# A convolution and attention-like layer pair on one core: first Toeplitz reads in sequence, channel 1's x in halves, filter weights scaled ahead

## The chip, the cores and the metric

One core of a Trainium2 chip. The metric is the device time of one execution in microseconds (us); before the change it is 943.02 (median of 3, 942.68 to 943.25).

## The reference

Input x is (4 images, 64 channels, 256, 256) in f32. Per channel, two layers follow each other.

```python
# layer 0: filters from a small net, separable, applied along both axes
h = sin(freq * (z @ w1 + b1)); h = sin(freq * (h @ w2 + b2)); h = sin(freq * (h @ w3 + b3))
h = (h @ wo) * decay                      # once with the X weights, once with the Y weights
k = einsum('ijk,imk->ijmk', hx, hy)       # causal 2-d convolution of x with k, by FFT
y = conv(x, k) + x * bias
# layer 1
scores = einsum('bpsd,bptd->bpst', y, y) / 16
out = batchnorm_over(b, s, d)(y + sum(scores * weights, -1, keepdims=True)) * gamma + beta
```

The sum over t of scores times weights is computed as a product of `weights` and y, then multiplied row by row with y and summed.

## The kernel before, in words

**Filters.** Three parameter transfers (`L315`) bring z, the weights, biases, frequencies and decays. TensorE makes layer 1 in two halves of 128 positions (`L645`). In each of the three layers VectorE forms `arg` of the first half from PSUM as (x + bias) * freq / 2 pi (`L780`) and ScalarE that of the second (`L506`); VectorE subtracts the nearest whole number of turns (`L788`, `L793`), ScalarE takes the sine (`L511`), and TensorE multiplies by the next weights (`L652`). A fourth product times the decay gives `filt` (`L800`). In front of each of the later products two filler matmuls (`keep_warm`, into `ps_c`, results unused) are issued, in front of the first four, and 24 after the filters are ready. SyncE stores `filt` to `pad_dram` (`L348`), waits, and reads it back as Toeplitz matrices: row p is the filter read from position p + 1 on. Channel 0 is read in two parts: S (f = 1, `first_s_landed`) and T (f = 0, `t_landed[0]`), each 128 KB (`L341`). Every other channel is one read of 256 KB (`L336`).

**Steady work.** The 4 images of a channel are 2 pairs; 64 channels make 128 steps. Every f32 operand is split in a high part (rounded by ScalarE) and a low part (subtraction, on GpSimd, or on VectorE for u). For pair n, TensorE forms U(n) (`ps_u`, x times S), Y(n) (`ps_z`, T times u) and C(n) (`ps_c`, weights times z). In step s it issues U(s-2), Y(s-3), C(s-4); each engine runs its own in-order stage with such lags. In the steps that matter here:

- SyncE issues, before the steps, xt of channel 0, w of channel 0, xt of channel 1, and after the filter store S and T; then the steps' loads: Toeplitz 1, w(1), x(0), xt(2), x(1), Toeplitz 2, and then w(2), which waits for the low part of w(0). x(n) is the x of pair n in natural layout, w(m) the layer 1 weights of channel m.
- ScalarE: xh of pairs 0 and 1 (`L548`), high parts of S (`L535`) and T (`L539`), uh(0) (`L519`), xh of pair 2, high part of Toeplitz 1, wh(0) (`L559`), uh(1), xh of pair 3, zh(0) (`L610`).
- GpSimd: xl of pair 0 (`L461`), low part of S (`L450`), xl of pair 1, low part of T (`L442`), xl of pair 2, low part of Toeplitz 1, wl(0) (`L474`), xl of pair 3, zl(0) (`L489`).
- VectorE: ul(0) (`L890`), ul(1), then z of pair 0 (`z_sb`, `L847`), which needs Y(0) and x(0).
- TensorE: U(0) needs the high part of S and xl of pair 0, U(1) xl of pair 1, Y(0) ul(0) and the low part of T; U(2) needs ul(1), the low part of Toeplitz 1 and xl of pair 2; C(0) needs wl(0) and zl(0).

Of the kernel before, what the change touches and what calls it, by code (L numbers as in the profile page):

```python
# [24 lines left out]
COL_BIAS, COL_FREQ = COL_W1 + P, COL_W1 + P + 3  # L25
COL_W2, COL_W3, COL_WO = (COL_FREQ + 1 + i * P for i in range(3))
COL_DECAY = COL_WO + P
# [9 lines left out]

WARM_FIRST, WARM_LAYER, WARM_TOEPLITZ = 4, 2, 24

# [71 lines left out]
def build(nc, x, xt, wt, params, out):  # L111
# [45 lines left out]
    with ExitStack() as ctx:  # L157
# [6 lines left out]
        def sem(name):  # L164
            return ctx.enter_context(nc.semaphore(name))
# [49 lines left out]
        filt = early[2][:, 0:PAD]  # L215
        arg, turns, part, hid = (early[3][:, i * SIDE:(i + 1) * SIDE] for i in range(4))


# [15 lines left out]
        hid_ready = sem("hid_ready")  # L234
        filt_ready = sem("filt_ready")
        filt_stored = sem("filt_stored")
        xt_landed = [sem(f"xt_landed{i}") for i in range(XR)]
# [61 lines left out]
        def z_parts(zs):  # L299
# [3 lines left out]
            return zh[:, zs.slot(2)], zl[:, zs.slot(2)]  # L303

        def u_bank(us):

            return ps_c if second_pair(us) else ps_u
# [4 lines left out]
        def _(sp):  # L312
            for start, end, landed in ((0, COL_W2, first_landed), (COL_W2, COL_DECAY, weights_landed),
                                       (COL_DECAY, NPARAM, rest_landed)):
                sp.dma_start(par[:, start:end], params[:, start:end]).then_inc(landed, 16)  # L315
# [22 lines left out]
            def load_first_toeplitz(f, landed):  # L338

                src = bass.AP(pad_dram, f * CH * PAD + 1, [[1, P], [1, SIDE]])  # L340
                sp.dma_start(toep_whole[:, 0, f, :], src).then_inc(landed, 16)  # L341

            load_xt(0, 0)
            load_w(0, 0)
            load_xt(1, 1)

# [51 lines left out]
        def _(pool):  # L398
            nc.gpsimd.memset(filt[:, 0:P], 0.0).then_inc(const_ready, 1)
            nc.gpsimd.memset(ones[:, :].bitcast(F32), 1.0 / P).then_inc(const_ready, 1)  # L400
            nc.gpsimd.memset(minus_half[:, :], -0.5).then_inc(const_ready, 1)
            nc.gpsimd.memset(everyone[:, :, 2 * P:2 * P + 2], P * BN_EPS).then_inc(const_ready, 1)
            pool.wait_ge(const_ready, 4)

# [27 lines left out]
            def stage(st):  # L432

                ms = st.trail(LAG_MEAN)
                if starts(ms) and not ending(ms, 4):
                    shift_means(ms)

                def low_toeplitz(ts, parts):
# [18 lines left out]

                if active(st):
                    wait(pool, xh_ready, st, 1)
                    r, h = st.ring(XR), st.half()  # L460
                    nc.gpsimd.tensor_tensor(xl[:, st.slot(4)], xt_sb[:, r, PAIR * h:PAIR * (h + 1), 0],  # L461
                                            xh[:, st.slot(4)].bitcast(F32), ALU.subtract)\
                        .then_inc(xl_ready, 1)

# [33 lines left out]
        def _(act):  # L498

            act.wait_ge(const_ready, 4)  # L500
            nc.scalar.activation(sine_loaded[:, :], minus_half[:, :], ACT.Sin)
            for layer in range(3):
                act.wait_ge(layer_done, 2 * layer + 2)
                if layer == 0:
                    act.wait_ge(bias_turns_ready, 1)
                nc.scalar.activation(arg[:, HALVES[1]], ps_u[:, 1, 0, 0:P], ACT.Identity,  # L506
                                     bias=bias_turns[:, layer:layer + 1], scale=freq_turns[:, 0:1])\
                    .then_inc(second_arg, 1)
                for i, half in enumerate(HALVES):
                    act.wait_ge(reduced, 5 * layer + 4 + 2 * i)  # L510
                    nc.scalar.activation(hid[:, half], part[:, half], ACT.Sin, scale=TWO_PI_BELOW)\  # L511
                        .then_inc(hid_ready, 1)

            def round_u(us):

                if active(us):
                    wait(act, u_done, us, 1)
                    wait(act, y_done, us, -1)
                    nc.scalar.activation(uh[:, us.slot(2)], u_bank(us)[:, :, :, :], ACT.Copy)\  # L519
                        .then_inc(uh_ready, 1)  # L520

            def stage(st):
# [19 lines left out]
                ts = toeplitz_step(st)  # L542
                if active(st):
                    r, h = st.ring(XR), st.half()
                    if h == 0:
                        act.wait_ge(xt_landed[r], st.turn(XR) * 16)
                    wait(act, u_done, st, -3)
                    nc.scalar.activation(xh[:, st.slot(4)], xt_sb[:, r, PAIR * h:PAIR * (h + 1), 0],  # L548
                                         ACT.Copy).then_inc(xh_ready, 1)

# [79 lines left out]
        def _(pe):  # L630
# [9 lines left out]

            pe.wait_ge(const_ready, 4)
            keep_warm(WARM_FIRST)
            pe.wait_ge(first_landed, 16)
            for i, half in enumerate(HALVES):
                mm(ps_u[:, i, 0, 0:P], par[:, COL_W1:COL_W1 + P],  # L645
                   par[:, COL_ZT + half.start:COL_ZT + half.stop], True, True).then_inc(layer_done, 1)
# [123 lines left out]
        def _(dve):  # L770
# [4 lines left out]
            nc.vector.tensor_scalar(bias_turns[:, :], par[:, COL_BIAS:COL_BIAS + 3], freq_turns[:, 0:1],  # L775
                                    None, ALU.mult).then_inc(bias_turns_ready, 1)
            for layer in range(3):

                dve.wait_ge(layer_done, 2 * layer + 1)
                nc.vector.tensor_scalar(arg[:, HALVES[0]], ps_u[:, 0, 0, 0:P],  # L780
                                        par[:, COL_BIAS + layer:COL_BIAS + layer + 1],
                                        freq_turns[:, 0:1], ALU.add, ALU.mult).then_inc(reduced, 1)
                for i, half in enumerate(HALVES):
                    if i == 0:
                        dve.wait_ge(reduced, 5 * layer + 2)
# [4 lines left out]
                    dve.wait_ge(reduced, 5 * layer + 3 + 2 * i)  # L790
# [6 lines left out]
            dve.wait_ge(const_ready, 4)  # L797
            for i in range(2):
                dve.wait_ge(layer_done, 7 + i)
                nc.vector.tensor_tensor(filt[:, P + P * i:P + P * (i + 1)], ps_u[:, i, 0, 0:P],  # L800
                                        par[:, COL_DECAY + P * i:COL_DECAY + P * (i + 1)], ALU.mult)\
                    .then_inc(filt_ready, 1)
# [248 lines left out]
```

## Time and profile before

| | |
|---|---|
| median of the runs | 943.02 us |
| profiled execution, its own time | 943.65 us |
| its span | 941.8 us |
| busy: TensorE, VectorE, ScalarE, GpSimd | 99%, 79%, 72%, 71% |
| HBM traffic | 259 GB/s over the span |
| transfers on SyncE's queue | 85.1% of the DMA engines' span |

The span runs from the first instruction to the last. A share of busy time is a mean over the whole span; the first 30 us look different from the rest and are read by themselves below. For a transfer the profile gives the time from its issue to its landing.

### The profile page before, as it was taken

The page shows a single profiled execution, that of the slowest core. Times are in us where ns is not written, and L with a number is a line of the kernel's source. Part 1 is how long each engine was busy: PE and PEld are TensorE (multiplying, and loading weights), DVE is VectorE, ACT ScalarE, POOL GpSimd, SP SyncE. Part 2 cuts the span into 40 slices and gives each one's busy share as a digit, 9 for nine tenths or more (in the row PEclk, how much of TensorE's full clock was granted, in tenths as well). Part 3 has the DMA queues.
Part 4 walks back from the last instruction along what each step waited for, and adds up shares of the span by engine and source line. Part 5 has one row for each costly group of instructions (what it writes and reads, how often), then busy time and mean ns, then how long its engine had stood idle before and what let it go on. Part 6 is the DMA issues. An engine that isn't in the chain of part 4 may idle for free.

```text
span 941.8 us, 18640 instructions
## 1 busy us (share of the span) xinstructions
PE 928.6 (99%) x5308; PEld 812.7 (86%) x5308; DVE 740.5 (79%) x2196; ACT 680.0 (72%) x1093; POOL 672.8 (71%) x526
## 2 busy tenths in 40 slices
PE   8999999999999999999999999999999999999995
PEld 6888888888888888888888888888888888888884
DVE  2778778878878878877887887887887878888787
ACT  4447777777777777777777777777677777777777
POOL 2777777777777767777777776876777776777763
PEclk9999999999999999999999999999999999999998
DMA  7778998898999999889799999979999999988945
GB/s 231 266 223 186 289 258 271 290 238 271 258 260 285 237 284 291 292 225 288 211 289 298 209 302 291 280 236 288 215 274 311 240 269 294 262 261 293 246 152 204
DMA packets 91454, 244.15 MB, mean 259 GB/s; under 512 B 17200, under 2 KB 41904, under 8 KB 83248
## 3 DMA queue, kind: packets, MB, share of 16 engines
q1 hardware_dynamic: 73440, 235.53, 85.1%
q10 hardware_dynamic: 18000, 8.46, 3.7%
q14 instruction: 9, 0.07, 0.0%
q8 instruction: 5, 0.08, 0.0%
HBM read 176.59 MB, written 67.37 MB: 259 GB/s over the span
## 4 chain that ended last, share of the span: by engine, by line
PE 95%; DVE 2%; DMA 1%; ACT 1%; issue 1%; POOL 0%; SPq 0%; POOLq 0%; DVEq 0%
PE ps_c L632 36%; PE ps_u L632 31%; PE ps_z L632 28%; DMA toep_whole<-filters_padded 1%; DVE z_sb L847 0%; DVE products L857 0%; POOL zl L489 0%; DMA filters_padded<-z_sb 0%; DVE ul L890 0%; ACT uh L519 0%; DVE z_sb L945 0%; DVE z_sb L780 0%; DVE stat L874 0%; DVE z_sb L793 0%; ACT zh L610 0%
## 5 line engine op out<-in xcount | busy, mean ns | idle before, releaser
L489 POOL TENSOR_TENSOR zl<-z_sb,zh 128x1024 fp32r<-128x1024 f32 x127 | 304.0, 2393 | 238.5 <-ACT zh L610 238.4
L857 DVE CUSTOM_DVE_ANT_0 products<-z_sb,ps_c 128x256 bf16<-128x256 f32 x504 | 182.3, 418 | 155.1 <-PE ps_c L632 155.1
L632 PE MATMUL ps_z<-uh,toep 128*128 128x512 f32 x768 | 271.4, 408 | 0.4 <-DVE z_sb L847 0.2
L585 ACT ACTIVATE out_sb<-z_sb,shift,gain 128x256 f32<-128x256 f32 x496 | 257.2, 591 | 5.5
L519 ACT ACTIVATE uh<-ps_u 128x1024 fp32r<-128x1024 f32 x127 | 130.6, 1028 | 174.4 <-PE ps_u L632 174.4
L632 PE MATMUL ps_u<-toep,xh 128*128 128x256 f32 x1016 | 234.8, 312 | 0.8 <-DVE ul L890 0.5
L632 PE MATMUL ps_c<-zh,wh 128*128 128x512 f32 x504 | 196.2, 389 | 0.1
L632 PE MATMUL ps_c<-zl,wh 128*128 128x512 f32 x504 | 196.1, 389 | 0.0
L632 PE MATMUL ps_c<-zh,wl 128*128 128x512 f32 x504 | 196.1, 389 | 0.0
L632 PE MATMUL ps_u<-toep_whole,xt_sb 128*128 128x128 f32 x1016 | 195.1, 273 | 0.0
L610 ACT ACTIVATE zh<-z_sb 128x1024 fp32r<-128x1024 f32 x127 | 134.7, 1061 | 63.6 <-DVE z_sb L847 54.3
L461 POOL TENSOR_TENSOR xl<-xt_sb,xh 128x512 fp32r<-128x512 f32 x128 | 166.5, 1301 | 11.6 <-ACT xh L548 11.6
L632 PEld LDWEIGHTS ps_u<-toep,xh 128*128 128x128 f32 x1016 | 163.0, 191 | 11.4 <-issue 0.9
L874 DVE BATCH_NORM_STATS2 stat<-z_sb 128x6 f32<-128x512 f32 x256 | 169.6, 707 | 0.1
L632 PEld LDWEIGHTS ps_z<-uh,toep 128*128 128x128 f32 x768 | 144.4, 188 | 29.0 <-issue 0.9
L890 DVE TENSOR_TENSOR ul<-ps_u,uh 128x1024 fp32r<-128x1024 f32 x127 | 154.6, 1217 | 14.8 <-ACT uh L519 14.6
L847 DVE SCALAR_TENSOR_TENSOR z_sb<-x_sb,par,ps_z 128x1024 f32<-128x1024 f32 x128 | 163.3, 1276 | 0.0
L632 PEld LDWEIGHTS ps_u<-toep_whole,xt_sb 128*128 128x128 f32 x1016 | 157.6, 191 | 0.0
L632 PE MATMUL ps_z<-ul,toep 128*128 128x512 f32 x384 | 149.9, 390 | 0.0
L632 PE MATMUL ps_u<-toep,xl 128*128 128x256 f32 x508 | 143.8, 283 | 0.0
L632 PEld LDWEIGHTS ps_c<-zh,wh 128*128 128x128 f32 x504 | 94.6, 188 | 20.4 <-issue 0.8
L632 PEld LDWEIGHTS ps_c<-zh,wl 128*128 128x128 f32 x504 | 94.6, 188 | 19.7
(95 smaller groups left out, 907.7 us busy)
## 6 DMA issues: line engine op xcount, KB each, us to landing
xt_sb<-xt_in SPq DMA_DIRECT2D x64, 1024.0 KB, 10.8
x_sb<-x_in SPq DMA_DIRECT2D x128, 512.0 KB, 8.9
out<-out_sb SPq DMA_DIRECT2D x124, 512.0 KB, 7.3
w_sb<-wt_in SPq DMA_DIRECT2D x64, 256.0 KB, 8.0
toep_whole<-filters_padded SPq DMA_DIRECT2D x63, 256.0 KB, 8.0
everyone<-partition_moments ACTq DMA_DIRECT2D x62, 128.0 KB, 8.5
out<-z_sb SPq DMA_DIRECT2D x2, 512.0 KB, 2.6
partition_moments<-own ACTq DMA_DIRECT2D x62, 1.0 KB, 7.0
```

Of the source, the lines that this page charges most:

```text
L461: nc.gpsimd.tensor_tensor(xl[:, st.slot(4)], xt_sb[:, r, PAIR * h:PAIR * (h + 1), 0], xh[:, st.slot(4)].bitcast(F32), ALU.subtract)\
L489: nc.gpsimd.tensor_tensor(low, z_sb[:, r, h], high.bitcast(F32), ALU.subtract)\
L519: nc.scalar.activation(uh[:, us.slot(2)], u_bank(us)[:, :, :, :], ACT.Copy)\
L585: last = nc.scalar.activation(to[:, k, b], z_sb[:, r, h, k, b], ACT.Identity, bias=shift[:, r, g:g + 1], scale=gain[:, r])
L610: nc.scalar.activation(z_parts(zs)[0], z_sb[:, r, h], ACT.Copy).then_inc(zh_ready, 1)
L632: return nc.tensor.matmul(o, a, b, start=start, stop=stop)
L847: nc.vector.scalar_tensor_tensor(out=z_sb[:, r, h].rearrange("p k b w -> p (k b w)"), in0=x_sb[:, zs.slot(4)].rearrange("p k b w -> p (k b ...
L857: return nc.vector.tensor_tensor_reduce(products[:, cs.slot(2), k, b], z_sb[:, r, h, k, b], bank[:, k, b], 1.0 / math.sqrt(SIDE), 0.0, ALU ...
L874: last = nc.vector.bn_stats(stat[:, r, h * BLOCKS + k], z_sb[:, r, h, k].rearrange("p b w -> p w b"))
L890: nc.vector.tensor_tensor(ul[:, us.slot(2)], u_bank(us)[:, :, :, :], uh[:, us.slot(2)].bitcast(F32), ALU.subtract)\
```

## The change

The filters' layers 2 and 3 no longer form `arg`. GpSimd multiplies their weights by freq / 2 pi per output column (`scaled`, from a new row of frequencies in the parameters) and makes a diagonal matrix of the biases in turns (from a new identity matrix). TensorE first multiplies that diagonal with a tile of ones into the layer's PSUM bank, then adds the scaled weights' product, so PSUM holds turns, and VectorE reads it twice. The layers alternate between `ps_u` and `ps_z`. The fillers in front of layers 2 and 3 go, those in front of the output product stay, those before the Toeplitz products become 15. The second parameter transfer grows to 256 KB, the third by 64 KB.

SyncE issues half of channel 1's xt (the images of pair 2) early, and waits for S before it issues T, Toeplitz 1, the other half of xt and w(0). ScalarE and GpSimd make xh and xl of pair 2 ahead of the Toeplitz parts; GpSimd also that of pair 1.

```diff
-COL_W2, COL_W3, COL_WO = (COL_FREQ + 1 + i * P for i in range(3))
+COL_W2, COL_W3, COL_FREQ_ROW, COL_EYE, COL_WO = (COL_FREQ + 1 + i * P for i in range(5))
-WARM_FIRST, WARM_LAYER, WARM_TOEPLITZ = 4, 2, 24
+WARM_FIRST, WARM_OUT, WARM_TOEPLITZ = 4, 2, 15
...
+        row_turns, unit = (early[1][:, i * P:(i + 1) * P] for i in range(2))
+        scaled = early[1][:, 2 * P:6 * P].rearrange("p (l k n) -> p l k n", l=2, k=2)
...
+        def layer_bank(layer, i):
+            return (ps_u, ps_z)[layer % 2][:, i, 0, 0:P]
...
-            for start, end, landed in ((0, COL_W2, first_landed), (COL_W2, COL_DECAY, weights_landed),
-                                       (COL_DECAY, NPARAM, rest_landed)):
+            for start, end, landed in ((0, COL_W2, first_landed), (COL_W2, COL_WO, weights_landed),
+                                       (COL_WO, NPARAM, rest_landed)):
...
             load_xt(0, 0)
-            load_w(0, 0)
-            load_xt(1, 1)
+            load_xt_half(1, 0, early_xt_landed)
...
             load_first_toeplitz(1, first_s_landed)
+            sp.wait_ge(first_s_landed, 16)
             load_first_toeplitz(0, t_landed[0])
+            load_toeplitz(1, 1)
+            load_xt_half(1, 1, xt_landed[1])
+            load_w(0, 0)
...
-                if starts(ts) and not first_channel(ts):
+                if starts(ts) and not (ts.static() and ts.channel() < 2):
                     wait(sp, u_done, ts, -2 * XR + 2)
                     load_toeplitz(ts.channel(), ts.ring(XR))
...
+            nc.gpsimd.memset(unit, 1.0).then_inc(const_ready, 1)
...
+            pool.wait_ge(weights_landed, 16)
+            nc.gpsimd.tensor_scalar(row_turns, par[:, COL_FREQ_ROW:COL_FREQ_ROW + P], 1.0 / (2.0 * math.pi),
+                                    None, ALU.mult).then_inc(row_turns_ready, 1)
+            pool.wait_ge(row_turns_ready, 1)
+            pool.wait_ge(bias_turns_ready, 1)
+            for i, col in enumerate((COL_W2, COL_W3)):
+                nc.gpsimd.tensor_scalar(scaled[:, i, 1], par[:, COL_EYE:COL_EYE + P], bias_turns[:, i + 1:i + 2],
+                                        None, ALU.mult).then_inc(scaled_ready, 1)
+                nc.gpsimd.tensor_tensor(scaled[:, i, 0], par[:, col:col + P], row_turns, ALU.mult)\
+                    .then_inc(scaled_ready, 1)
...
+                if st.static() and st.number() == 1:
+                    low_x(st)
+                    low_x(Step(0, 2))
...
+                if st.static() and st.number() == 1:
+                    high_x(Step(0, 2))
...
-            pe.wait_ge(weights_landed, 16)
-            for layer, col in enumerate((COL_W2, COL_W3, COL_WO)):
-                keep_warm(WARM_LAYER)
+            for layer in (1, 2):
+                pe.wait_ge(scaled_ready, 2 * layer - 1)
+                for i in range(2):
+                    mm(layer_bank(layer, i), scaled[:, layer - 1, 1], unit, True, False)
+                pe.wait_ge(scaled_ready, 2 * layer)
                 for i, half in enumerate(HALVES):
-                    pe.wait_ge(hid_ready, 2 * layer + 1 + i)
-                    mm(ps_u[:, i, 0, 0:P], par[:, col:col + P], hid[:, half], True, True)\
+                    pe.wait_ge(hid_ready, 2 * layer - 1 + i)
+                    mm(layer_bank(layer, i), scaled[:, layer - 1, 0], hid[:, half], False, True)\
                         .then_inc(layer_done, 1)
+            keep_warm(WARM_OUT)
+            pe.wait_ge(rest_landed, 16)
+            for i, half in enumerate(HALVES):
+                pe.wait_ge(hid_ready, 5 + i)
+                mm(layer_bank(3, i), par[:, COL_WO:COL_WO + P], hid[:, half], True, True).then_inc(layer_done, 1)
...
             for layer in range(3):
-                dve.wait_ge(layer_done, 2 * layer + 1)
-                nc.vector.tensor_scalar(arg[:, HALVES[0]], ps_u[:, 0, 0, 0:P],
-                                        par[:, COL_BIAS + layer:COL_BIAS + layer + 1],
-                                        freq_turns[:, 0:1], ALU.add, ALU.mult).then_inc(reduced, 1)
                 for i, half in enumerate(HALVES):
+                    if layer == 0:
...
+                        whole = arg[:, half]
                     else:
-                        dve.wait_ge(second_arg, layer + 1)
-                    nc.vector.tensor_scalar(turns[:, half], arg[:, half], ROUND_MAGIC, ROUND_MAGIC,
+                        dve.wait_ge(layer_done, 2 * layer + 1 + i)
+                        whole = layer_bank(layer, i)
+                    nc.vector.tensor_scalar(turns[:, half], whole, ROUND_MAGIC, ROUND_MAGIC,
                                             ALU.add, ALU.subtract).then_inc(reduced, 1)
...
-                    nc.vector.tensor_tensor(part[:, half], arg[:, half], turns[:, half], ALU.subtract)\
+                    nc.vector.tensor_tensor(part[:, half], whole, turns[:, half], ALU.subtract)\
                         .then_inc(reduced, 1)
```

## Rows read from the trace of the kernel before

**Rows 1.** The page: TensorE's and other engines' busy time; granted clock in 40 slices.
```profile
PE 928.6 (99%) x5308; PEld 812.7 (86%) x5308; DVE 740.5 (79%) x2196; ACT 680.0 (72%) x1093; POOL 672.8 (71%) x526
...
PEclk9999999999999999999999999999999999999998
```
**Rows 2.** Waits of TensorE, 30 to 930 us: total, times, longest.
```profile
PE ps_z L632 <- DVE z_sb L847: 0.2, 1, 0.2
```
**Rows 3.** Chain that ended last, first 50 us: start, duration, what.
```profile
5.55 0.81 PE ps_u L632 x2
6.39 0.42 DVE z_sb L780
6.83 0.24 DVE z_sb L788
...
11.09 0.30 DVE z_sb L800
11.41 2.06 DMA filters_padded<-z_sb
...
14.34 7.50 DMA toep_whole<-filters_padded
...
25.10 1.28 DVE z_sb L847
...
30.10 2.98 PE ps_c L632 x12
```
**Rows 4.** Timeline of GpSimd, 0 to 45 us.
```profile
0.88 0.20 POOL L400 MEMSET ones<- 128x128 f32 x1
...
17.52 0.73 POOL L450 TENSOR_TENSOR toep<-toep_whole,toep 128x256 fp32r<-128x256 f32 x1 [5.06 <-ACT toep L535]
...
22.98 1.31 POOL L442 TENSOR_TENSOR toep<-toep_whole,toep 128x512 fp32r<-128x512 f32 x1
```
**Rows 5.** DMA issues one by one, parameters 2, S, T, Toeplitz 1, w(1), x(0): us to landing last.
```profile
par<-params_in SPq DMA_DIRECT2D x1, 192.0 KB, 2.6
...
toep_whole<-filters_padded SPq DMA_DIRECT2D x1, 128.0 KB, 3.5
...
toep_whole<-filters_padded SPq DMA_DIRECT2D x1, 128.0 KB, 4.3
...
toep_whole<-filters_padded SPq DMA_DIRECT2D x1, 256.0 KB, 7.5
...
w_sb<-wt_in SPq DMA_DIRECT2D x1, 256.0 KB, 7.7
...
x_sb<-x_in SPq DMA_DIRECT2D x1, 512.0 KB, 8.5
```
**Rows 6.** Timeline of SyncE's queue: start and length of the issues.
```profile
0.75 1.33 SPq L315 DMA_DIRECT2D par<-params_in  x3
...
13.49 0.81 SPq L341 DMA_DIRECT2D toep_whole<-filters_padded  x2
...
14.82 0.47 SPq L328 DMA_DIRECT2D w_sb<-wt_in  x1
15.33 0.43 SPq L323 DMA_DIRECT2D x_sb<-x_in  x1
```
**Rows 7.** Timeline of ScalarE, 16 to 62 us.
```profile
17.03 0.42 ACT L535 ACTIVATE toep<-toep_whole 128x256 fp32r<-128x256 f32 x1 [5.47 <-DMA toep_whole<-filters_padded]
...
22.40 0.62 ACT L559 ACTIVATE wh<-w_sb 128x512 fp32r<-128x512 f32 x1
```
**Rows 8.** Timeline of TensorE: first matmul of U(0), last of Y(0).
```profile
17.50 0.39 PE L632 MATMUL ps_u<-toep,xh 128*128 128x256 f32 x1 [0.32 <-ACT toep L535]
...
24.47 0.40 PE L632 MATMUL ps_z<-uh,toep 128*128 128x512 f32 x1
```
**Rows 9.** Timeline of TensorE: the first four fillers and the 24.
```profile
1.22 2.07 PE L632 MATMUL ps_c<-ones 128*128 128x512 f32 x4 [1.22 <-POOL everyone L402]
...
11.44 5.74 PE L632 MATMUL ps_c<-ones 128*128 128x512 f32 x24 [0.38 <-DVE z_sb L800]
```

More of the change, by code:

```diff
@@ L235, in build @@
         filt_ready = sem("filt_ready")
+        row_turns_ready = sem("row_turns_ready")
+        scaled_ready = sem("scaled_ready")
+        early_xt_landed = sem("early_xt_landed")
         filt_stored = sem("filt_stored")
@@ L341, in load_first_toeplitz, with load_xt_half @@
                 sp.dma_start(toep_whole[:, 0, f, :], src).then_inc(landed, 16)
+            def load_xt_half(m, h, landed):
+                images = slice(PAIR * h, PAIR * (h + 1))
+                sp.dma_start(xt_sb[:, m, images, :, :].rearrange("p b k h -> p (b k h)"),
+                             xt[m, :, images, :, :].rearrange("p b k h -> p (b k h)"))\
+                    .then_inc(landed, 16)
             load_xt(0, 0)
-            load_w(0, 0)
-            load_xt(1, 1)
+            load_xt_half(1, 0, early_xt_landed)
             sp.wait_ge(filt_ready, 2)
@@ L400, in _ @@
             nc.gpsimd.memset(ones[:, :].bitcast(F32), 1.0 / P).then_inc(const_ready, 1)
+            nc.gpsimd.memset(unit, 1.0).then_inc(const_ready, 1)
             nc.gpsimd.memset(minus_half[:, :], -0.5).then_inc(const_ready, 1)
             nc.gpsimd.memset(everyone[:, :, 2 * P:2 * P + 2], P * BN_EPS).then_inc(const_ready, 1)
-            pool.wait_ge(const_ready, 4)
+            pool.wait_ge(const_ready, 5)
+            pool.wait_ge(weights_landed, 16)
[8 more added lines that the diff above has]
+                    .then_inc(scaled_ready, 1)
             def shift_means(ms):
@@ L436, in stage, with low_x @@
                     shift_means(ms)
+                def low_x(xs):
+                    wait(pool, xh_ready, xs, 1)
+                    r, h = xs.ring(XR), xs.half()
+                    nc.gpsimd.tensor_tensor(xl[:, xs.slot(4)], xt_sb[:, r, PAIR * h:PAIR * (h + 1), 0],
+                                            xh[:, xs.slot(4)].bitcast(F32), ALU.subtract).then_inc(xl_ready, 1)
                 def low_toeplitz(ts, parts):
@@ L456, in stage @@
                         low_toeplitz(ts, slice(0, 2))
[L458 to L463, printed above, removed]
+                if active(st) and not (st.static() and 1 <= st.number() <= 2):
+                    low_x(st)
                 if starts(ts) and first_channel(ts):
@@ L498, in _ @@
         def _(act):
-            act.wait_ge(const_ready, 4)
+            act.wait_ge(const_ready, 5)
             nc.scalar.activation(sine_loaded[:, :], minus_half[:, :], ACT.Sin)
+            act.wait_ge(layer_done, 2)
+            act.wait_ge(bias_turns_ready, 1)
+            nc.scalar.activation(arg[:, HALVES[1]], layer_bank(0, 1), ACT.Identity, bias=bias_turns[:, 0:1],
+                                 scale=freq_turns[:, 0:1]).then_inc(second_arg, 1)
             for layer in range(3):
[L503 to L508, printed above, removed]
                 for i, half in enumerate(HALVES):
-                    act.wait_ge(reduced, 5 * layer + 4 + 2 * i)
+                    act.wait_ge(reduced, 4 * layer + 4 + 2 * i)
                     nc.scalar.activation(hid[:, half], part[:, half], ACT.Sin, scale=TWO_PI_BELOW)\
@@ L520, in round_u, with high_x @@
                         .then_inc(uh_ready, 1)
+            def high_x(xs):
+                r, h = xs.ring(XR), xs.half()
+                if xs.static() and xs.number() == 2:
+                    act.wait_ge(early_xt_landed, 16)
+                elif h == 0 or xs.static() and xs.number() == 3:
+                    act.wait_ge(xt_landed[r], xs.turn(XR) * 16)
+                wait(act, u_done, xs, -3)
+                nc.scalar.activation(xh[:, xs.slot(4)], xt_sb[:, r, PAIR * h:PAIR * (h + 1), 0],
+                                     ACT.Copy).then_inc(xh_ready, 1)
             def stage(st):
@@ L542, in stage @@
                 ts = toeplitz_step(st)
[L543 to L549, printed above, removed]
+                if active(st) and not (st.static() and st.number() == 2):
+                    high_x(st)
+                if st.static() and st.number() == 1:
+                    high_x(Step(0, 2))
                 if starts(ts):
@@ L639, in keep_warm @@
                     mm(ps_c[:, 0], ones[:, :], ones[:, :].unsqueeze(1).broadcast_to([P, SIDE * PAIR // P, P]), True, True)
-            pe.wait_ge(const_ready, 4)
+            pe.wait_ge(const_ready, 5)
             keep_warm(WARM_FIRST)
@@ L644, in _ @@
             for i, half in enumerate(HALVES):
-                mm(ps_u[:, i, 0, 0:P], par[:, COL_W1:COL_W1 + P],
+                mm(layer_bank(0, i), par[:, COL_W1:COL_W1 + P],
                    par[:, COL_ZT + half.start:COL_ZT + half.stop], True, True).then_inc(layer_done, 1)
-            pe.wait_ge(weights_landed, 16)
-            for layer, col in enumerate((COL_W2, COL_W3, COL_WO)):
-                keep_warm(WARM_LAYER)
+            for layer in (1, 2):
[3 more added lines that the diff above has]
+                pe.wait_ge(scaled_ready, 2 * layer)
                 for i, half in enumerate(HALVES):
-                    pe.wait_ge(hid_ready, 2 * layer + 1 + i)
-                    mm(ps_u[:, i, 0, 0:P], par[:, col:col + P], hid[:, half], True, True)\
+                    pe.wait_ge(hid_ready, 2 * layer - 1 + i)
+                    mm(layer_bank(layer, i), scaled[:, layer - 1, 0], hid[:, half], False, True)\
                         .then_inc(layer_done, 1)
+            keep_warm(WARM_OUT)
[3 more added lines that the diff above has]
+                mm(layer_bank(3, i), par[:, COL_WO:COL_WO + P], hid[:, half], True, True).then_inc(layer_done, 1)
             pe.wait_ge(filt_ready, 2)
@@ L776, in _ @@
                                     None, ALU.mult).then_inc(bias_turns_ready, 1)
+            dve.wait_ge(layer_done, 1)
+            nc.vector.tensor_scalar(arg[:, HALVES[0]], layer_bank(0, 0), par[:, COL_BIAS:COL_BIAS + 1],
+                                    freq_turns[:, 0:1], ALU.add, ALU.mult).then_inc(reduced, 1)
             for layer in range(3):
-                dve.wait_ge(layer_done, 2 * layer + 1)
-                nc.vector.tensor_scalar(arg[:, HALVES[0]], ps_u[:, 0, 0, 0:P],
-                                        par[:, COL_BIAS + layer:COL_BIAS + layer + 1],
-                                        freq_turns[:, 0:1], ALU.add, ALU.mult).then_inc(reduced, 1)
@@ L783, in _ @@
                 for i, half in enumerate(HALVES):
-                    if i == 0:
-                        dve.wait_ge(reduced, 5 * layer + 2)
-                    else:
-                        dve.wait_ge(second_arg, layer + 1)
-                    nc.vector.tensor_scalar(turns[:, half], arg[:, half], ROUND_MAGIC, ROUND_MAGIC,
+                    if layer == 0:
+                        if i == 0:
+                            dve.wait_ge(reduced, 2)
+                        else:
+                            dve.wait_ge(second_arg, 1)
+                        whole = arg[:, half]
+                    else:
+                        dve.wait_ge(layer_done, 2 * layer + 1 + i)
+                        whole = layer_bank(layer, i)
@@ L789, in _ @@
+                    nc.vector.tensor_scalar(turns[:, half], whole, ROUND_MAGIC, ROUND_MAGIC,
                                             ALU.add, ALU.subtract).then_inc(reduced, 1)
-                    dve.wait_ge(reduced, 5 * layer + 3 + 2 * i)
+                    dve.wait_ge(reduced, 4 * layer + 3 + 2 * i)
                     if layer > 0:
                         dve.wait_ge(hid_ready, 2 * layer - 1 + i)
-                    nc.vector.tensor_tensor(part[:, half], arg[:, half], turns[:, half], ALU.subtract)\
+                    nc.vector.tensor_tensor(part[:, half], whole, turns[:, half], ALU.subtract)\
@@ L794, in _ @@
                         .then_inc(reduced, 1)
             dve.wait_ge(rest_landed, 16)
-            dve.wait_ge(const_ready, 4)
+            dve.wait_ge(const_ready, 5)
             for i in range(2):
                 dve.wait_ge(layer_done, 7 + i)
-                nc.vector.tensor_tensor(filt[:, P + P * i:P + P * (i + 1)], ps_u[:, i, 0, 0:P],
+                nc.vector.tensor_tensor(filt[:, P + P * i:P + P * (i + 1)], layer_bank(3, i),
                                         par[:, COL_DECAY + P * i:COL_DECAY + P * (i + 1)], ALU.mult)\
@@ L1036 @@
         params[ORDER:P, COL_BIAS + i] = a["L0_conv_Y" + name].reshape(-1)
+    for i, half in enumerate("XY"):
+        cols = slice(ORDER * i, ORDER * (i + 1))
+        params[:, COL_FREQ_ROW:COL_FREQ_ROW + P][:, cols] = a[f"L0_conv_{half}freq"].reshape(1, -1)
+    params[:, COL_EYE:COL_EYE + P] = np.eye(P)
     params[:, COL_DECAY:COL_DECAY + SIDE] = decay_rows(ch)
```

## The prediction

> **What bounds the kernel now.** I read the page first: TensorE is busy for 99% of the span, next to VectorE's 79% [rows 1]. The waits of TensorE between 30 and 930 us come next: one line, 0.2 us in all [rows 2]. From 30 us on the kernel is one unbroken row of matmuls, and nothing in the diff touches a matmul, a shape or a wait of a steady step. What remains is what lies before 30.1 us, where the chain of waits [rows 3] runs through other engines: three filter layers (mm, `L780` scale and bias, `L788`/`L793` range reduction, `L511` sine), the store of the filters (11.41 to 13.47), Toeplitz reads, then `ul`, `z_sb` and zl of pair 0, until TensorE starts the first C product at 30.10 and never stops again. So the question is one number: by how much the start of C(0), at 30.10, moves. That shift, and nothing else, is the change of the total. The sum is made in the profiled execution (span 941.8, its own time 943.65); the median is 943.02, 0.63 lower, and I put the shift on the median. About 0.2% of it, 1.9 us, is what a measurement can tell from no change.
>
> **Filter layers.** Layers 2 and 3 lose the arg pass: 6.39 to 6.83 is 0.44 us each [rows 3], 0.88 for both. Now `turns` reads PSUM. A two-input pass from PSUM of the same size takes 0.30 (`L800`), the `L780` pass from PSUM 0.42, against 0.24 for `L788` from SBUF; I take 0.30 (same size, no scalar pointers), so +0.06 on each `turns` that lies on the path, three or four of them, some 0.2 (0.18 each, 0.7, at the upper bound; 0 at the lower). What is added sits on GpSimd and TensorE. The second of the three parameter transfers issued from 0.75 to 2.08 went out at about 1.2 and landed 2.6 later, at 3.8 [rows 5, 6]; it grows from 192 to 256 KB, say 4.0. GpSimd then runs one scale, one diagonal, one weight product before layer 2 may start. Its price is not in the trace for 128x128: between the 0.20 of a memset of this size and the 0.73 of a 128x256 subtraction; with the 1.31 of 128x512 the line through both sizes gives 0.44 [rows 4]. Two at 0.44: diagonal at 4.9; three: weights at 5.3, before the first sine is done, which lets the layer 2 matmul go at 5.55 [rows 3]. The two bias matmuls occupy TensorE for some 0.8 (the 0.81 pair [rows 3]): 4.9 to 5.7, against 5.55 when layer 2 began. Slip 0.15 (0 with GpSimd at 0.20 each; 0.7 at 0.73 each). Layer 3's bias and weights (6.2 on GpSimd) are ready while VectorE reduces layer 2, so cost nothing; without that cover they would cost 0.8. Layer 1 is unchanged, the last layer's weights come with the third transfer, two microseconds before their use. The larger parameters (128 KB more) stand before channel 0's transfer, whose xh is off the chain. Sum: 0.88 - 0.2 - 0.15, some **0.55 to 0.6 earlier**: store issued at 10.8, landed at 12.9 by its 2.06. The queue ahead of it is lighter (w of channel 0 and half of xt of channel 1, 768 KB, now go behind the reads), so I add nothing.
>
> **First read alone.** Before, S (the f=1 read) was issued at 13.49 and took 3.5, to 17.0, with T (about 13.9) and channel 1's 256 KB (14.34) issued behind it [rows 3, 5, 6]. Alone its bounds are the store's 2.06 for 192 KB below and 3.5 above. I take 2.3, since these are 128 overlapping 1 KB rows and the issue-to-landing of 192 KB from DRAM was 2.6 among others: 12.9 + 2.3 = **15.2, 1.8 earlier**. ACT's high part takes 0.42 [rows 7], so U(0) starts at 15.65 instead of 17.50 [rows 8]. GpSimd no longer has xl of pairs 1 and 2 between the low parts; each is a 128x512 subtraction of 1.3 [rows 4], now done in the wait for S, and it frees GpSimd but gives TensorE nothing by itself, which waited for ACT and VectorE there. U(0), U(1) and Y(0) took from 17.50 to 24.9 [rows 8]; they end at 23.0.
>
> **T, channel 1 and w behind it.** SP now waits for S; queued behind that wait are T, channel 1's Toeplitz rows, half of xt, w(0), and all loads of the steps (w(1), x(0), xt(2), x(1), ...). T, issued at 15.2, alone in front: 2.3 again, 17.5 (before 18.2). ACT needs it before uh(0), which can start at 18.3: hidden, with 0.4 for its high part. The Trainium skill ("DMA: Bandwidth & Descriptors", Anatomy of one DMA) puts a fixed cost of about 2 us on every transfer, mostly its completion, and so speaks against any wait between two. By it, as an estimate, S and T would land at 15.2 and 17.5; the row of the store agrees (2.06), and this second latency is in the sum with the effect that T still arrives before uh(0).
>
> Channel 1's rows landed 3.6 after T before (21.84 against 18.2 [rows 3, 5]). The least is what the queue needs: w(1), the same 256 KB, landed 0.7 after them (14.82 + 7.7), x(0) 1.3 after that (15.33 + 8.5) [rows 5, 6]. I take the middle, 2.1, since fewer competitors stand around: 19.6. Then come half of xt, 512 KB like x(0), 1.3, and w(0), 0.7: **w(0) lands at 21.6**. This is the term that decides. On ACT the order is toep (channel 1), wh(0) `L559`, uh(1) `L519`; before, w had long landed and wh began at 22.40, `z_sb` 2.70 later at 25.10, C(0) 5.0 after that [rows 3, 7]. Now wh begins with w(0), 21.6; ul(1) ends and `z_sb` of pair 0 starts at 24.3; C(0) at 29.3. x(0), w(1) and itself behind w(0), lands 2.0 after it, 23.6, under the 2.7. So of 1.85 won at U(0), 1.05 is given back as idle before uh(1): **shift -0.8, 942.2**.
>
> **Filler matmuls.** 24 in 5.74 us filled 11.44 to 17.2 [rows 9]; 15 at that rate are 3.6, from 10.8 to 14.4, before U(0) at 15.65: no cost, and S is the cover. The page shows a granted clock near full from the first slice [rows 1], yet the first four took 2.07 together [rows 9], 0.52 each: the lower level, 1.2 GHz, and the later ones 0.24 each, the 2.4 GHz level. The two fillers in front of each of layers 2 and 3 go. If the level has not risen by 10.8, fifteen cost up to 15 x 0.52 = 7.8, to 18.6.
>
> **Rivals.**
> (A) Full gain, **941.0** (940.6 to 941.2): Toeplitz reads spaced apart no longer slow each other, channel 1 lands within 0.85 of T, w(0) by 20.35, and `z_sb` waits only for Y(0) at 23.0. C(0) at 28.1, -2.0; with S in 2.06, -2.3. For it: the row S 3.5 against the larger store's 2.06. Against: 1.5 MB of loads follow in the same burst. Chance 0.25.
> (B) Gain at S eaten, **943.0**: channel 1 lands 2.9 after T, at 20.4, w(0) at 22.4, and wh begins where it did, whatever U(0) won. For it: 2.9 lies between the 0.7 and 3.6 of the rows. Chance 0.17.
> (C) Slower, **944.8**: w(0) becomes the late load. All upper bounds: S 3.5 (16.4), T 2.3 (18.7), channel 1 3.6 later (22.3), w(0) 24.3, wh then, C(0) at 32.0, +1.9. It loses as soon as w(0) lands after 22.4, one for one. For it: each of the three transfers issued from 14.34 to 15.33 took 7.5 us or more [rows 5]. Against: it needs all slow ends together to pass 944.9. Chance 0.13, half of it beyond.
> (D) The clock: fillers outlast the read, U(0) starts at 18.6, +1.1, and if U(0) and U(1) (some 5 us) ran at the lower level as much as 5 more: **944 to 948**. The Trainium skill ("TensorE: Matmul & The Clock Gate", HAM oscillation) has the array fall back to the half rate when it waits long; by that rule the gap from 14.4 to 15.65, and the thinner layers, count against the change. Against: bias matmuls take the fillers' place in the layers, and the gap to come is 1.3 us in a stretch where TensorE is otherwise busy. Chance 0.05.
> (E) GpSimd's first scale costs more than an instruction of its size: its first subtraction showed none. It delays layer 2 one for one, and 1 us of it gives 943.2. Chance 0.02.
> The forecast itself has 0.38, its own range 941.3 to 943.0.
>
> **The numbers.** Faster than 941.1 comes from A (0.20) and a tail of the forecast (0.02): 0.22. Slower than 944.9 from half of C (0.06) and most of D (0.04): 0.10. The rest, 0.68, is within 0.2%. The range 940.8 to 943.9 leaves out D, the upper part of C and the fastest of A, about 0.17.
>
> **What would show it.** The steps: store issued near 10.8; S 2.3 from issue to landing; U(0) at 15.65; wh(0) directly behind w(0)'s landing, with ACT's idle time in front of `wh` put down to that transfer; `z_sb` at 24.3; C(0) at 29.3; no waits of TensorE later. Wrong if uh(1) is released by U(1) and not by wh (then A), if fillers still run when S lands (D), or if TensorE shows new gaps after 30 us, which nothing here allows.

## The result, and the profile after

The changed kernel takes 948.95 us (median of 6 runs, 948.23 to 949.3), the one before 943.05 (median of 6): 5.9 us more, ratio 1.0063, 95% interval 1.0053 to 1.0073. The profiled execution took 948.54, with a span of 946.6 against 941.8. I had said 942.2, and 943.9 at most.

The steady steps did not change, as forecast. TensorE's waits from 30 to 930 us are the one of [rows 2] again. The loss of 4.8 in the span is complete when C(0) starts, at 34.95 instead of 30.10. The medians differ by 5.9, about 1 us more than the two spans: the profiled execution of the kernel before lies 0.6 above its median, that of the changed one 0.4 below. Below are lines of the chain that ended last, first 60 us (start, duration, what); compare [rows 3]:

```profile
3.99 0.55 POOL z_sb L424
...
4.62 0.61 POOL z_sb L429
...
5.28 2.08 PE ps_z L673 x8
...
11.25 1.89 DMA filters_padded<-z_sb
...
13.16 2.84 DMA toep_whole<-filters_padded
...
17.38 7.58 DMA w_sb<-wt_in
...
24.98 0.63 ACT wh L600
25.61 0.92 ACT uh L552
...
26.56 1.23 DVE ul L941
...
27.93 4.61 PE ps_u L673 x20
32.54 2.58 PE ps_z L673 x9
35.12 2.72 PE ps_c L673 x12
```

Read it from the middle. The chain now passes through the transfer of w(0), 7.58 us long, into wh, uh(1) and ul(1). Then U(2) takes 4.61 us, where the later ones of this chain take 2.32, and Y(1) 2.58 with half of it slow. ScalarE's timeline shows which waits stand before uh(1) (compare [rows 7]):

```profile
16.03 0.42 ACT L579 ACTIVATE toep<-toep_whole 128x256 fp32r<-128x256 f32 x1 [4.11 <-DMA toep_whole<-filters_padded]
18.95 0.42 ACT L583 ACTIVATE toep<-toep_whole 128x256 fp32r<-128x256 f32 x1 [2.51 <-DMA toep_whole<-filters_padded]
19.28 1.01 ACT L552 ACTIVATE uh<-ps_u 128x1024 fp32r<-128x1024 f32 x1
23.05 0.63 ACT L583 ACTIVATE toep<-toep_whole 128x512 fp32r<-128x512 f32 x1 [2.76 <-DMA toep_whole<-filters_padded]
24.98 0.63 ACT L600 ACTIVATE wh<-w_sb 128x512 fp32r<-128x512 f32 x1 [1.31 <-DMA w_sb<-wt_in]
25.52 1.00 ACT L552 ACTIVATE uh<-ps_c 128x1024 fp32r<-128x1024 f32 x1
```

U(1) was done by 21.4, and uh(1) was ready to run then. It stands behind the high part of Toeplitz 1 (started 23.05) and wh (started 24.98) in ScalarE's order. TensorE meanwhile has nothing to do from the end of Y(0) at 24.0 until 27.93. Its waits in the first 45 us, the first line:

```profile
PE ps_u L673 <- DVE ul L941: 3.9, 1, 3.9
```

What that gap does to the clock shows in the windows (us of the stretch, busy us and instructions of TensorE, its weight loads, VectorE, ScalarE, GpSimd; then the granted clock, DMA share, GB/s):

```profile
26.00:26.50 0.50, 0.00 (x0) 0.00 (x0) 0.00 (x0) 0.50 (x2) 0.50 (x1) 1.00 0.96 401
26.50:27.00 0.50, 0.00 (x0) 0.00 (x0) 0.44 (x1) 0.50 (x2) 0.46 (x1) 0.68 1.04 434
...
28.00:33.00 5.00, 5.00 (x22) 4.90 (x23) 2.28 (x3) 1.48 (x2) 2.75 (x2) 0.50 1.02 350
33.00:33.50 0.50, 0.50 (x2) 0.40 (x2) 0.00 (x0) 0.50 (x2) 0.00 (x0) 0.50 0.88 360
33.50:34.00 0.50, 0.50 (x3) 0.40 (x3) 0.37 (x1) 0.50 (x2) 0.00 (x0) 1.00 0.96 401
```

In the idle gap the granted clock falls from 1.00 to 0.50 (1.2 GHz), and U(2) and most of Y(1) run at it until 33.5. The Trainium skill ("TensorE: Matmul & The Clock Gate", HAM oscillation) describes this: a wait for data lets the clock gate drop, and the next products start cold; the trace agrees, with 4.61 against 2.32 for a U product.

Where the transfers land, asked one by one for S, T, Toeplitz 1, half of xt, w(0) and x(0) (KB, us from issue to landing; compare [rows 5]):

```profile
toep_whole<-filters_padded SPq DMA_DIRECT2D x1, 128.0 KB, 2.8
...
toep_whole<-filters_padded SPq DMA_DIRECT2D x1, 128.0 KB, 2.9
...
toep_whole<-filters_padded SPq DMA_DIRECT2D x1, 256.0 KB, 6.6
...
xt_sb<-xt_in SPq DMA_DIRECT2D x1, 512.0 KB, 7.4
...
w_sb<-wt_in SPq DMA_DIRECT2D x1, 256.0 KB, 7.6
...
x_sb<-x_in SPq DMA_DIRECT2D x1, 512.0 KB, 7.7
```

S landed 1.0 earlier than before, T 0.7 later, Toeplitz 1 (issued 16.39) 1.2 later, and w(0) (issued 17.38) at 24.96, 2.5 after wh had begun in the kernel before.

### The profile page after: what moved, and what is told of

It reads as the page before. It is cut to its first block, busy times and chain, and to the rows that moved or that the text cites. A ratio compares the mean times of both kernels' runs of the same rounds, so it can differ in the third digit from the quotient of the medians.

```text
span 946.6 us, 18637 instructions
## 1 busy us (share of the span) xinstructions
PE 928.2 (98%) x5303; PEld 814.4 (86%) x5303; DVE 740.2 (78%) x2194; ACT 679.1 (72%) x1091; POOL 674.8 (71%) x532
## 4 chain that ended last, share of the span: by engine, by line
PE 95%; DMA 2%; DVE 1%; issue 0%; ACT 0%; POOL 0%; SPq 0%; POOLq 0%; DVEq 0%
PE ps_c L673 36%; PE ps_u L673 32%; PE ps_z L673 28%; DMA w_sb<-wt_in 1%; DMA toep_whole<-filters_padded 0%; DMA par<-params_in 0%; DVE products L908 0%; DVE ul L941 0%; ACT uh L552 0%; DMA filters_padded<-z_sb 0%; DVE z_sb L996 0%; DVE z_sb L898 0%; DVE stat L925 0%; ACT wh L600 0%; POOL z_sb L429 0%
## 5 line engine op out<-in xcount | busy, mean ns | idle before, releaser
L673 PEld LDWEIGHTS ps_c<-zl,wh 128*128 128x128 f32 x504 | 94.6, 188 | 19.6
```

Source lines behind the costliest of these rows:

```text
L673: return nc.tensor.matmul(o, a, b, start=start, stop=stop)
```

## Experiments

They ran in three groups, each on a chip of its own and with its own runs of the kernel before: 1, 2, 4 and 5 (median of before 943.15), 6, 8, 11 and 12 (943.01), 3, 7, 9 and 10 (943.25). Across groups the ratios are compared, not the microseconds. "C(0)" is the start of the first C product in the timeline of the profiled execution. Span minus C(0) is 911.5 to 911.8 in all of them but one (912.4, named below), so within that execution the shift of C(0) is the whole difference. One execution is not the median, though: in 1, 5, 10, 11 and 12 the profiled one issued the filter store at 10.27 to 10.74, in all others at 11.25 to 11.60, for reasons that the edits do not explain (see the last section). Their C(0) is early by up to about a microsecond for that alone, and the medians decide.

| kernel | median us | ratio to before, 95% interval | span | C(0) |
|---|---|---|---|---|
| before | 943.05 | | 941.8 | 30.10 |
| changed | 948.95 | 1.0063 (1.0053, 1.0073) | 946.6 | 34.95 |
| 1 changed, w(0) early | 946.63 | 1.0041 (1.0027, 1.0055) | 942.4 | 30.68 |
| 2 changed, TensorE kept busy in the gap | 946.65 | 1.0038 (1.0024, 1.0052) | 944.7 | 32.93 |
| 3 changed, wh(0) behind uh(1) | 946.39 | 1.0038 (1.0024, 1.0052) | 944.4 | 32.77 |
| 4 changed, no wait for S | 944.31 | 1.0011 (1.0002, 1.0020) | 942.7 | 30.89 |
| 5 before, with the wait for S | 945.11 | 1.0022 (1.0012, 1.0032) | 943.0 | 31.48 |
| 6 filter part alone | 944.09 | 1.0016 (1.0007, 1.0026) | 941.7 | 29.93 |
| 7 filter part alone, 24 fillers | 943.89 | 1.0007 (0.9997, 1.0016) | 942.0 | 30.23 |
| 8 changed, w early, no wait | 944.03 | 1.0014 (1.0004, 1.0023) | 943.2 | 31.42 |
| 9 as 8, 24 fillers | 943.30 | 1.0000 (0.9990, 1.0009) | 941.8 | 30.05 |
| 10 as 9, wh(0) behind uh(1) | 943.49 | 1.0005 (0.9996, 1.0015) | 940.8 | 29.03 |
| 11 as 1, burst held for Toeplitz 1 | 949.64 | 1.0074 (1.0058, 1.0091) | 945.3 | 32.89 |
| 12 as 8, burst held for Toeplitz 1 | 944.48 | 1.0018 (1.0008, 1.0027) | 942.1 | 30.27 |

**The theory** after the result: w(0) lands late, ScalarE's order carries that to uh(1), and the gap drops the clock. **The rivals**: the Toeplitz reads alone, or the filter part, or traffic that slows the matmuls.

**1. w(0) early.**
```diff
             load_xt_half(1, 0, early_xt_landed)
+            load_w(0, 0)
...
             load_xt_half(1, 1, xt_landed[1])
-            load_w(0, 0)
```


> The changed kernel, with w of channel 0 loaded early again. Late-w theory: ScalarE's wh(0) starts when the high part of Toeplitz 1 is done (about 23.6 instead of 24.98), uh(1) at 24.1, ul(1) and the z of pair 0 about 1.4 earlier, at 26.3; with the idle gap of TensorE then 2.5 instead of 3.9 us, its clock may stay at the 2.4 GHz level, which gives 2.4 more: about 945.1 us; if the clock falls all the same, 947.5. Rival, the Toeplitz reads alone set it and w is not late on the path: no change, 948.9.

946.63. The profiled run took 944.52, the four others 946.36 to 947.46 with mean clocks of 0.993 to 0.995 against its 0.997. In the profiled one wh follows the high part of Toeplitz 1 with no wait, and TensorE waits 2.5 us for ul(1) instead of 3.9:

```profile
22.43 0.63 ACT L583 ACTIVATE toep<-toep_whole 128x512 fp32r<-128x512 f32 x1 [2.77 <-DMA toep_whole<-filters_padded]
22.97 0.61 ACT L600 ACTIVATE wh<-w_sb 128x512 fp32r<-128x512 f32 x1
```

The chain of that run no longer passes through w or ul(1); z of pair 0 waits for x(0), and C(0) with it:

```profile
17.21 8.44 DMA x_sb<-x_in
25.67 1.29 DVE z_sb L898
```

The granted clock of that run stayed at 1.00. w's place is on the path, and the two outcomes of the expectation, 945.1 and 947.5, both occur nearly as given, with the lower mean clock the more frequent; the four others have no trace, so that it fell in the same gap there is argued from the times and the mean clocks.

**2. TensorE kept busy.** Sixteen fillers into an unused bank behind Y(0); nothing else changes.
```diff
                 if active(zs):
                     product_y(zs)
+                if st.static() and st.number() == 3:
+                    for _ in range(16):
+                        mm(ps_avg[:, 0], ones[:, :], ones[:, :].unsqueeze(1).broadcast_to([P, SIDE * PAIR // P, P]), True, True)
```


> The changed kernel with 16 filler matmuls into an unused bank behind Y(0), so that TensorE is busy in the gap of 3.9 us before U(2). Clock theory: U(2) still starts at 27.9, but U(2) and Y(1) run at 2.4 GHz, and C(0) starts when zl(0) is done, at 32.6 instead of 34.95: 2.4 less, 946.5 us. Rival, the slow matmuls of 27.9 to 33.5 come from traffic and not from the idle gap: 948.9.

946.65, as expected, 2.3 less. w(0) is as late (wh at 25.21), yet the clock stays at full and C(0) starts when zl(0) is there:

```profile
28.00:30.00 2.00, 1.97 (x17) 1.87 (x17) 1.97 (x4) 0.76 (x1) 0.65 (x1) 1.00 1.01 367
30.00:32.00 2.00, 2.00 (x14) 1.74 (x13) 0.75 (x2) 1.55 (x3) 1.62 (x1) 1.00 1.02 330
```

The DMA rates are those of the changed kernel (367 and 330 GB/s, there 350 from 28 to 33), so traffic is not what made the matmuls slow. With TensorE busy in the gap and nothing else changed, this shows that the idle gap is what lowered the clock.

**3. wh(0) behind uh(1).** Transfers as in the changed kernel; ScalarE makes wh(0) one step later.
```diff
                 if filling:
                     round_u(st.trail(LAG_U))
+                if st.static() and st.number() == 3:
+                    act.wait_ge(w_landed[0], 16)
+                    nc.scalar.activation(wh[:, 0], w_sb[:, 0], ACT.Copy).then_inc(wh_ready, 1)
...
-                if starts(ws):
+                if starts(ws) and not first_channel(ws):
```


> The changed kernel; only ScalarE's wh(0) moves behind uh(1), all transfers stay. If the late w(0) costs because uh(1) stands behind it in ScalarE's order: uh(1) right after the high part of Toeplitz 1, at 23.6 instead of 25.5, U(2) at 26.1, gap 2.1 us, clock mostly held; z of pair 0 then waits for x(0), at 26.9, C(0) at 31.9: about 945.7 us. Rival, the clock falls all the same: 947.5 or more.

946.39: between the two. uh(1) now follows the high part of Toeplitz 1 directly, and TensorE's gap is 2.3 us:

```profile
24.34 1.01 ACT L552 ACTIVATE uh<-ps_c 128x1024 fp32r<-128x1024 f32 x1
25.73 0.63 ACT L573 ACTIVATE wh<-w_sb 128x512 fp32r<-128x512 f32 x1 [0.39 <-DMA w_sb<-wt_in]
```

U(2) starts at 26.75 instead of 27.93, but the clock fell in this run too, with the shorter gap: U(2) takes 3.86 us instead of 2.32, and the window from 28 to 30 shows a granted clock of 0.50.

```profile
26.75 3.86 PE ps_u L676 x20
```
```profile
28.00:30.00 2.00, 2.00 (x12) 2.00 (x11) 1.97 (x3) 1.00 (x1) 0.95 (x1) 0.50 1.00 366
```

The fall came late here: in the window from 26.7 to 27.5, U(2)'s first, the granted clock is still 1.00, and from 27.5 to 28 it is 0.63. C(0) started at 32.77 and not at 31.9. So ScalarE's order, not a need for w, carried the delay of w(0) to uh(1); and the read of Toeplitz 1 is next in line.

**4 and 5. The wait for S**, taken out of the changed kernel and put into the one before:
```diff
             load_first_toeplitz(1, first_s_landed)
-            sp.wait_ge(first_s_landed, 16)
             load_first_toeplitz(0, t_landed[0])
```


> The changed kernel without SyncE's wait for S; order of the loads as changed. If the wait is what pushed the reads and w(0) back: S takes 3.5 again (U(0) 0.6 later, at 17.1), T, Toeplitz 1 and w(0) are issued 2.4 earlier and w(0) lands 1 to 2 us earlier, at 23 to 24; uh(1) moves with it, the clock may hold: 944.5 to 947.5. Rival, the order alone makes w late and the wait costs nothing: 948.9.

> The kernel before with only SyncE's wait for S added. If the wait costs by itself: S lands 0.7 earlier, T 0.9 later, Toeplitz 1 1.3 to 2 us later (23.2 to 24), and uh(1), z of pair 0 and C(0) with it: 944.4 to 945; over 946 if TensorE's clock falls in the longer gap. Rival, serial reads are faster each and nothing is lost: 943.0 or less.

944.31, 4.6 less than changed and just under the expected range; and 945.11, 2.0 more than before (943.15, median of 19) and just over it. The wait costs alone, without w's new place. Without the wait (4) the chain still runs through w(0), which lands at 23.15, but TensorE waits only 1.3 us for ul(1) and the granted clock stays at 1.00. In the kernel with it added, SyncE's queue and the landings of S, T and Toeplitz 1:

```profile
13.25 3.46 SPq L341 DMA_DIRECT2D toep_whole<-filters_padded  x2
16.75 0.43 SPq L336 DMA_DIRECT2D toep_whole<-filters_padded  x1
```
```profile
toep_whole<-filters_padded SPq DMA_DIRECT2D x1, 128.0 KB, 3.1
...
toep_whole<-filters_padded SPq DMA_DIRECT2D x1, 128.0 KB, 2.9
...
toep_whole<-filters_padded SPq DMA_DIRECT2D x1, 256.0 KB, 6.5
```

S gains 0.4 of its 3.5 from being alone. T and Toeplitz 1 are issued 2.4 later, and by their shorter durations they get only 1.4 and 1.0 of that back. Toeplitz 1 lands at 23.2 instead of 21.84, TensorE waits 2.4 us for ul(1) instead of 0.5, and C(0) moves by 1.4, in an execution in which S was issued 0.2 earlier than in the one before (13.25 against 13.49).

**6 and 7. The filter part alone**, with 15 and with 24 fillers before U(0). The load order and ScalarE's and GpSimd's orders are those of before; 7 differs from 6 by one number:
```diff
-WARM_FIRST, WARM_OUT, WARM_TOEPLITZ = 4, 2, 15
+WARM_FIRST, WARM_OUT, WARM_TOEPLITZ = 4, 2, 24
```


> The changed filter layers, parameters and fillers (15), with the load order, ScalarE's and GpSimd's order of before. If the filter part is nearly neutral, as the trace after says (store issued at 11.25 against 11.41): store 0.2 earlier at best, C(0) 0.2 earlier, 942.9 us, within 0.5. Rival, the filter part has a share of the loss, by GpSimd's late diagonal or by the clock: 943.5 or more.

> The filter part alone, with 24 fillers before U(0) again instead of 15. filters_only lost 1.1 us, and half of its executions had a lower mean clock. If that is TensorE's idle time before U(0), 2.2 us with 15 fillers, its slow half goes and its clock is 0.996 or more in nearly all runs: 943.2 to 943.8 us. Rival, the bias matmuls and GpSimd's steps are the loss: 944.1 again, with the same spread.

944.09 and 943.89. Of the ten runs of 6, six lie between 943.78 and 944.28 at mean clocks of 0.996 or 0.997, four between 945.08 and 945.78 at 0.994: the rival's side, not the expected 942.9. With 24 fillers all ten lie between 943.48 and 944.52, none below 0.995, but their median is 0.1 above the expected range. TensorE's wait before U(0), with 15 and with 24:

```profile
PE ps_u L663 <- ACT toep L571: 2.2, 1, 2.2
```
```profile
PE ps_u L663 <- ACT toep L571: 0.6, 1, 0.6
```

So nine fillers fewer go with about 1.6 us more in four of ten executions, and with 0.9 thousandths (0.8 us) in the ratios. The two ran on different chips and their intervals overlap; what supports the reading is that none of the 25 runs of the kernel before beside 6, which has 24 fillers, is below 0.995 either. The filter part itself shows no gain: its interval holds 1 (0.9997 to 1.0016), its centre is 0.6 us above.

**8, 9 and 10. What remains when the losses are undone.** 8 joins edits 1 and 4; 9 has 24 fillers as well; 10 adds edit 3.

> The changed kernel without the wait for S and with w of channel 0 early; what is left of the change is the filter part, xh and xl of pair 2 ahead, Toeplitz 1 explicit and half of xt behind it. If wait and w are the whole loss, less than before is left: 942.6 to 943.2 us. Rival, a third part costs too: 944 or more.

> Changed kernel without the wait for S, with w of channel 0 early and 24 fillers. If wait, w order and the missing fillers are all of the loss: 942.8 to 943.3 us, all runs at a clock of 0.996 or more. Rival, the remaining filter part costs over half a microsecond: 943.7 or more.

> As a_fixed, with wh(0) behind uh(1) as well. uh(1) may start with the end of U(1); but z of pair 0 waits for Y(0), so it gains 0 to 0.4 us: 942.5 to 943.2. Rival, nothing to gain or wl(0) becomes late: equal to a_fixed or more.

944.03, 943.30, 943.49: the rival's side for 8, as expected for 9, and for 10 no gain, as its rival said. In the profiled run of 8 the clock fell at the end of the gap of 2.2 us before U(0) (17.36), and U(0) took 4.16 us instead of 2.6:

```profile
16.00:17.30 1.30, 0.00 (x0) 0.00 (x0) 0.00 (x0) 0.41 (x1) 0.00 (x0) 1.00 0.96 65
17.30:18.50 1.20, 1.14 (x5) 1.14 (x6) 0.00 (x0) 0.01 (x1) 0.73 (x1) 0.55 1.04 231
```

With 24 fillers no loss is left: 1.0000 (0.9990 to 1.0009), all runs at 0.995 or more. The rest of the change, taken together, is neutral here within that interval, 0.9 us either way: half of xt behind the reads, xh and xl ahead, Toeplitz 1 issued by name, and the filter part. None of the three is faster than the kernel before. The low C(0) of 10, 29.03, comes from a profiled run whose filter store was issued at 10.46; its median is not lower.

**11 and 12. Is the read of Toeplitz 1 slow by its company?** The burst waits for it:
```diff
             load_toeplitz(1, 1)
+            sp.wait_ge(t_landed[1], 16)
             load_xt_half(1, 1, xt_landed[1])
```


> The changed kernel with w of channel 0 early and with SyncE waiting for Toeplitz 1 as well before it issues half of xt and the steps' loads. If the burst behind it is what makes the read of Toeplitz 1 take 6.6 us: it lands 3 to 3.5 after its issue, near 19.5, uh(1) follows U(1), z of pair 0 at 23.8 or with x(0), C(0) near 29: 942 us. Rival, the read is slow by itself: it lands at 22.5 again, x(0) only near 27, 945 to 947.

> As the last, but SyncE waits for Toeplitz 1 before the burst. S, T and Toeplitz 1 run beside each other alone. If the burst slows them: S 3.5, T 4.5 and Toeplitz 1 at 18.5 to 19 instead of 21.2, z of pair 0 limited by Y(0) at 24.5 or by x(0), which is issued at 20: 942.5 to 943. Rival, reads are slow by themselves: x(0) lands late, 945 or more.

949.64, above both figures of its expectation, and 944.48, between the two. In 11, with only T beside it, Toeplitz 1 takes 5.0 us (15.45 to 20.46) instead of 6.6, not the 3 to 3.5 expected: the burst is 1.6 of it. In 12, beside S and T, it takes 4.86. It landed 4.1 after T in the changed kernel and 2.3 after it in 11 (T at 18.2), so the burst is 1.8 of that distance. But x(0), held back with the burst, lands at 27.9 in 11 and becomes the new wait, as the rival said:

```profile
15.45 5.01 DMA toep_whole<-filters_padded
...
21.33 6.55 DMA x_sb<-x_in
...
27.91 1.29 DVE z_sb L899
```

In 12 the read of Toeplitz 1 is short as well, and x(0) lands at 25.25, later than z needs it:

```profile
13.33 4.86 DMA toep_whole<-filters_padded
```

The span of 11 holds 0.6 more after C(0) than the others, and its other three runs took 949.6 to 950.5, over what its profiled one (947.51) shows. Both stay unexplained, so only the landings are read from 11.

## Why the prediction was wrong

**What held.** The frame held: within an execution the time is the start of C(0) plus a constant, and no steady step changed. The chain from w(0) to z held too: z of pair 0 was to start 2.7 after wh; it started at 27.70, with wh at 24.98. I had named w(0) as "the term that decides", the point from which it loses (22.4), and its loss "one for one": 24.96 is 2.6 past it, and U(2) began 2.6 later than before. The spacing of the queue held: half of xt landed 1.3 after Toeplitz 1, and w(0) 0.7 after that. The fillers ended before S landed, as said.

**The landing of w(0), 21.6 against 24.96.** Four terms came out late, one of them by far. The filter part was to give 0.55 to 0.6 (the terms written there add up to 0.53) and gave 0.16 (store issued at 11.25): GpSimd's scale and diagonal took 0.54 and 0.60, not 0.44, and the bias pair held TensorE longer than the 0.8 assumed (with the layer's own products, eight passes, 2.08), so that layer 2's first half reached VectorE at 6.96 instead of 6.39, which ate what the dropped `arg` passes saved. `turns` from PSUM was right, 0.29. S alone was to take 2.3 and took 2.84: the store of 192 KB, 1.89 here, was the wrong row to go by for 128 KB read back in overlapping rows; whether the overlap or the direction makes the difference no run tests. T took 2.9, not 2.3. The section of the Trainium skill cited beside T ("DMA: Bandwidth & Descriptors", Anatomy of one DMA) has its figures from transfers issued by GpSimd, while these go by SyncE's queue. And Toeplitz 1 came 4.1 after T, where I took 2.1, the middle between 0.7 and 3.6, "since fewer competitors stand around". That was the first failing step, and the largest term of the late landing. The competitors were there, because everything had been queued behind the wait and was issued at once: with that burst held back (11) Toeplitz 1 came 2.3 after T, close to the 2.1. The read still took 5.0 from issue to landing there, with only T beside it. Sum: 0.2 (store landed at 13.1, not 12.9) + 0.5 + 0.6 + 2.0 = 3.3, of the 3.4 missed.

**The second failing step: what the clock does after the gap.** No case of mine had it. Rival C stopped at 944.8 (943.02 and its 1.9 are 944.9), because I let C(0) follow z after a fixed 5.0. It came 7.25 after z. I had looked for the clock only at the fillers before U(0) (rival D) and gave that 0.05. The gap that mattered was the one I made myself in the forecast, "given back as idle before uh(1)": here it was 3.9 us, the clock fell in it, and the next 5.5 us of matmuls run at half speed, 2.3 us by experiment 2. By the terms of my own late case, w(0) at 24.3, the gap would have been near 3 us. I priced idle time as idle time and nothing more. The two steps account for C(0): 29.3 forecast, 34.95 measured, of which z of pair 0 is 3.4 late and the clock 2.3. The other 1.0 of the miss is the distance of the two profiled executions from their medians, which I had taken as the same before and after.

**The fillers.** I held 15 for enough since they would end at 14.4 against U(0) at 15.65. They ended at 15.0 with U(0) at 16.50. By 6 against 7, and 8 against 9 (ratio 1.0014 to 1.0000), "no cost" was wrong in some of the executions; in the changed kernel itself the fillers were not tried alone.

**The parts of the 5.9 us**, as far as these runs separate them: the clock in the gap 2.3 (experiment 2); the wait for S 2.0 (alone, in the kernel before); w's place, through ScalarE's order, the 1.3 that wh waits for w(0) with what the longer gap adds; the fillers 0.8 by 6 and 7 and 1.3 by 8 and 9, each across two chips and with intervals about as wide as the effect. They overlap: taking out the wait alone gives back 4.6, w early alone 2.3, and both together 4.9, because each of them closes the same gap. Whether the filter part costs the 0.6 that its centre shows is open; experiment 9, which contains it, is level with before. What xh and xl ahead give by themselves was not tried.

## What to carry to other kernels

An added wait on the queue that issues transfers delays the issue of all that stands behind it, here by 2.4 us, while the transfer it protects gained 0.4 to 0.7; count the last of the queue, not the first. A load that is moved back must be followed through the in-order engine that consumes it: the copy of w stood in front of a copy that did not need it. And an idle gap of TensorE in a dense kernel is to be priced with what the clock does after it, here 2.3 us on top of a gap of 3.9. Last, a landing can depend on what is issued behind a transfer: the burst behind Toeplitz 1 was 1.6 of its 6.6 us.

## What the runs showed of the hardware

The same filter layers end at two times in different executions of nearly the same code: the store was issued at 11.41 in the profiled execution of the kernel before and at 10.74 with the wait for S added, which cannot act on them. The chains differ in the matmul pairs of the filter layers, 0.81 at 5.55 in the one [rows 3] and 0.50 in the other, as if TensorE had reached its faster level earlier; the windows give 1.00 for both, so this is argued and not shown:

```profile
5.50 0.50 PE ps_u L633 x2
```

The changed layers show it as well (stores at 11.25 to 11.60 and at 10.27 to 10.57).

Idle gaps of TensorE of 2.2 to 2.5 us lowered the clock in some profiled executions (3 with 2.3 before U(2), 8 with 2.2 before U(0)) and not in others (1 with 2.5, 5 with 2.4, 6 with 2.2). The gap of 3.9 lowered it in the profiled one, and all six runs of the changed kernel have a mean clock of 0.992 or 0.993. For both effects a single profile can mislead: experiment 1's shows 942.4 of span, 2.2 to 3.1 less than its four other runs.
